# The attention's projections, values and output projection, each issued as two halves in neighbouring rounds

## The reference

```python
x = L0_attn_x
x = x + _L0_attn_ref(_layernorm(x, axis=-1), ...)   # softmax attention, 16 heads of 8 channels
x = x + _L0_ffn_ref(_layernorm(x, axis=-1), ...)    # ternary weights, 128 -> 512 -> 512 -> 512 -> 128
x = x + _L1_attn_ref(_layernorm(x, axis=-1), ...)   # gated linear attention, 8 heads, a scan over tokens
x = x + _L1_ffn_ref(_layernorm(x, axis=-1), ...)    # router, 3 of 8 experts per sequence
```

```python
Q = x @ wq + bq; K = x @ wk + bk; V = x @ wv + bv
Q = Q.reshape(B * H, S, D); K = K.reshape(B * H, S, D); V = V.reshape(B * H, S, D)
scores = jnp.einsum('bqd,bkd->bqk', Q, K) / jnp.sqrt(jnp.float32(D))
attn = jax.nn.softmax(scores, axis=-1)
ctx = jnp.einsum('bqk,bkd->bqd', attn, V).reshape(B, S, E)
out = ctx @ wo + bo
out = out + x
```

## Time and profile before

| | |
|---|---|
| Median of 3 runs | 1133.3 us (1132.64, 1133.3, 1139.46) |
| The profiled execution's own time | 1130.58 us |
| Its span in the profile | 1128.7 us |
| TensorE busy | 1018.0 us (90%) |
| ScalarE busy | 823.8 us (73%) |
| VectorE busy | 642.6 us (57%) |
| GpSimd busy | 369.6 us (33%) |
| Granted TensorE clock, mean | 0.97 of full |

### The profile page before, as it was taken

How to read it: one execution, slowest core, us unless ns; L and a number is a source line. 1 busy time by engine, 2 the same in 40 slices (tenths; PEclk the granted TensorE clock), 3 DMA queues, 4 the chain that set the end, 5 groups by cost and what they waited for, 6 DMA issues and landing times.

```text
span 1128.7 us, 16760 instructions
## 1 busy us (share of the span) xinstructions
PE 1018.0 (90%) x5970; PEld 508.5 (45%) x5970; DVE 642.6 (57%) x1173; ACT 823.8 (73%) x1108; POOL 369.6 (33%) x317
## 2 busy tenths in 40 slices
PE   2799999999999999999697888788588899999998
PEld 1233333333333333333275555465255536666667
DVE  3121444526344444313453899999999999986200
ACT  2599999999999999999457577566667576555541
POOL 1000010101000010100143677898678755755100
PEclk8699999999999999999899899899899999999999
DMA  5765462635455462610101101000000111111200
GB/s 126 121 121 110 82 119 61 123 66 105 78 104 97 85 107 53 119 35 15 33 1 36 33 8 39 29 10 19 19 27 12 57 57 44 41 48 29 63 22 20
DMA packets 99677, 66.91 MB, mean 59 GB/s; under 512 B 62532, under 2 KB 85860, under 8 KB 97508
## 3 DMA queue, kind: packets, MB, share of 16 engines
q1 hardware_dynamic: 99552, 65.34, 27.9%
q10 hardware_dynamic: 24, 0.25, 0.1%
HBM read 46.41 MB, written 18.87 MB: 58 GB/s over the span
## 4 chain that ended last, share of the span: by engine, by line
PE 64%; DVE 15%; ACT 6%; POOL 5%; issue 4%; SPq 3%; DMA 3%; ACTq 0%; DVEq 0%; POOLq 0%
PE PS L1458 26%; PE PS L1443 15%; PE PS L1629 6%; DVE R L1270 6%; PE PS L1618 5%; PE PS L1492 3%; POOL R L871 3%; DVE R L1261 3%; SPq L788 2%; PE PS L1387 1%; DVE RB L1223 1%; PE PS L1532 1%; PE PS L1556 1%; PE PS L1565 1%; PE PS L1373 1%
## 5 line engine op out<-in xcount | busy, mean ns | idle before, releaser
L908 ACT ACTIVATE R<-PS 128x1024 f32<-128x1024 f32 x512 | 474.4, 1085 | 61.4 <-PE PS L1443 60.7
L1458 PE MATMUL PS<-R 128*32 128x512 f32 x2048 | 315.2, 610 | 1.4 <-issue 1.4
L871 POOL TENSOR_TENSOR R<-R 128x512 f32<-128x512 f32 x128 | 212.3, 1674 | 55.5 <-DVE R L1270 30.1
L1270 DVE TENSOR_TENSOR_SCAN R<-R 128x512 f32<-128x512 f32 x128 | 209.2, 1635 | 0.0
L1443 PE MATMUL PS<-RA 34*128 34x512 f32 x1024 | 190.0, 449 | 19.2 <-DMA RA<-QD 18.6
L1492 PE MATMUL PS<-RB,WR 128*128 128x512 f32 x640 | 172.4, 413 | 20.5 <-DVE R L1229 12.5
L1443 PEld LDWEIGHTS PS<-RA 34*128 34x128 f32 x1024 | 77.5, 187 | 216.3 <-issue 194.5
L1492 PEld LDWEIGHTS PS<-RB,WR 128*128 128x128 f32 x640 | 120.9, 192 | 64.9 <-DVE R L1229 14.5
L1458 PEld LDWEIGHTS PS<-R 128*32 128x32 f32 x2048 | 68.0, 108 | 106.2 <-issue 94.2
L857 POOL TENSOR_TENSOR RB<-R,RB 128x512 fp32r<-128x512 f32 x48 | 74.8, 1562 | 83.3 <-ACT RB L918 73.9
L847 POOL PARTITION_ALL_REDUCE R<-R x8 | 3.0, 374 | 290.6 <-DVE R L1110 290.6
(11 more groups left out here) (139 smaller groups left out, 1041.3 us busy)
## 6 DMA issues: line engine op xcount, KB each, us to landing
RA<-QD SPq DMA_DIRECT2D x256, 64.0 KB
QD<-RA SPq DMA_DIRECT2D x128, 64.0 KB, 2.1
RA<-QD SPq DMA_DIRECT2D x64, 128.0 KB
OD<-R SPq DMA_DIRECT2D x128, 32.0 KB, 2.1
R<-OD SPq DMA_DIRECT2D x128, 32.0 KB
VD<-RC SPq DMA_DIRECT2D x16, 256.0 KB, 2.2
RC<-VD SPq DMA_DIRECT2D x128, 32.0 KB
WP<-in_Wa SPq DMA_DIRECT2D x12, 256.0 KB, 3.1
```

The source lines that it names most:

```text
L871: pool.tensor_tensor(st, st, Qc[b % 2], ALU.mult).then_inc(S["qh"], 1)
L908: act.activation(PR[u % 4], bank(2 * s, 1024), ACT.Exp, scale=SC).then_inc(S["exp"], 1)
L1270: dve.tensor_tensor_scan(st, Ac[k], st, CS[:, v:v + 1] if k else 0.0, ALU.mult, ALU.add).then_inc(S["scanned"], 1)
L1458: op = pe.matmul(bank(ob)[c:c + 32, :], VAF[b % 2][:, at:at + 32], PR[u % 4][:, 512 * h:512 * h + 512], start=(j == 0), stop=(j == 7), til ...
```

## The change

Each of the three larger side steps becomes two. The first half is a new step that stands one round before the old one (keys 4, 10, 13 and 18 before keys 5, 11, 14 and 19), with the waits; the second half stays at the old key, writes the rest of the same bank and signals VectorE as before. The Q and K projections are cut at column 256, the values at group 4 of 8, the output projection after 2 of its 4 parts. Where the steps stand outside the rounds (block 0's preparation, block 7's closing) the two halves follow each other directly.

```diff
--- before.py
+++ after.py
@@ -137,8 +137,11 @@
 
         return {
             3: lambda bk: self.add("turn_in", b, bk, self.xn[b]),
+            4: lambda bk: self.add("split_1", b, 1, bk),
             5: lambda bk: (self.add("split", b, 1, bk), self.add("keep", b, 1, 0, 4)),
+            10: lambda bk: self.add("split_1", b, 0, bk),
             11: lambda bk: (self.add("split", b, 0, bk), self.add("keep", b, 0, 0, 4)),
+            13: lambda bk: self.add("values_1", b, bk),
             14: lambda bk: (self.add("values", b, bk), self.add("flag", b)),
             15: lambda bk: self.add("load_pair", 4 * b),
             16: lambda bk: self.add("load_pair", 4 * b + 1),
@@ -168,6 +171,7 @@
 
         return {
             13: lambda bk: self.add("divide", b),
+            18: lambda bk: self.add("project_1", b, bk),
             19: project,
             21: residual,
             23: norm,
@@ -179,8 +183,10 @@
         self.add("pads", 0)
         self.norm_in(0)
         self.add("turn_in", 0, 1, self.xn[0])
+        self.add("split_1", 0, 1, 2)
         self.add("split", 0, 1, 2)
         self.add("keep", 0, 1, 0, 1)
+        self.add("split_1", 0, 0, 3)
         self.add("split", 0, 0, 3)
         self.add("keep", 0, 0, 0, 1)
         for w in (1, 0):
@@ -190,6 +196,7 @@
             self.add("keep", 0, w, 2, 4)
         for n in (1, 2, 3):
             self.add("load_pair", n)
+        self.add("values_1", 0, 4)
         self.add("values", 0, 4)
         self.add("flag", 0)
         self.add("pads", 1)
@@ -453,9 +460,10 @@
     def stream_a(self):
 
         last = self.close(7)
-        for key in (13, 19, 21, 23, 27):
+        for key in (13, 18, 19, 21, 23, 27):
             last[key](6)
-            yield
+            if key != 18:
+                yield
 
 
     def rest(self):
@@ -1380,23 +1388,35 @@
                 transpose4(XN[b % 3], bk).then_inc(S["xt_ps"], 1)
                 emptied[bk] = ("xt", b + 1)
 
-            def split(b, w, bk):
+            def split_1(b, w, bk):
                 need.wait_ge("small_in", 64)
                 need.wait_ge("xt", b + 1)
                 room(bk)
-                pe.matmul(bank(bk), wA[:, w, :], xtblock(b), start=True, stop=True).then_inc(S["qk_ps"], 1)
+                pe.matmul(bank(bk, 256), wA[:, w, :], xtblock(b)[:, 0:256], start=True, stop=True)
+
+            def split(b, w, bk):
+                pe.matmul(bank(bk)[:, 256:512], wA[:, w, :], xtblock(b)[:, 256:512], start=True,
+                          stop=True).then_inc(S["qk_ps"], 1)
                 emptied[bk] = ("qk_f", split_no(b, w))
 
-            def values(b, bk):
+            def values_of(b, bk, g):
+                t0 = 512 * b + 64 * g
+                for c in range(2):
+                    op = pe.matmul(bank(bk)[64 * c:64 * c + 64, 64 * g:64 * g + 64], XT[:, t0:t0 + 64],
+                                   view(wA[:, 2, :], (16, 8), (1, 8), at=8 * c), start=True, stop=True,
+                                   tile_position=(0, 64 * c))
+                return op
+
+            def values_1(b, bk):
                 need.wait_ge("small_in", 64)
                 need.wait_ge("xt", b + 1)
                 room(bk)
-                for g in range(8):
-                    t0 = 512 * b + 64 * g
-                    for c in range(2):
-                        op = pe.matmul(bank(bk)[64 * c:64 * c + 64, 64 * g:64 * g + 64], XT[:, t0:t0 + 64],
-                                       view(wA[:, 2, :], (16, 8), (1, 8), at=8 * c), start=True, stop=True,
-                                       tile_position=(0, 64 * c))
+                for g in range(4):
+                    values_of(b, bk, g)
+
+            def values(b, bk):
+                for g in range(4, 8):
+                    op = values_of(b, bk, g)
                 op.then_inc(S["v_ps"], 1)
                 emptied[bk] = ("va", b + 1)
 
@@ -1462,13 +1482,19 @@
             def finish(pr):
                 emptied[6 + pr % 2] = ("ctx_copied", pr + 1)
 
-            def project(b, bk):
-                k = b % 2
+            def project_of(b, bk, i):
+                return pe.matmul(bank(bk)[:, 128 * i:128 * i + 128], CT[b % 2][:, 128 * i:128 * i + 128], wA[:, 3, :],
+                                 start=True, stop=True)
+
+            def project_1(b, bk):
                 need.wait_ge("ctx", b + 1)
                 room(bk)
-                for i in range(4):
-                    op = pe.matmul(bank(bk)[:, 128 * i:128 * i + 128], CT[k][:, 128 * i:128 * i + 128], wA[:, 3, :],
-                                   start=True, stop=True)
+                for i in range(2):
+                    project_of(b, bk, i)
+
+            def project(b, bk):
+                for i in range(2, 4):
+                    op = project_of(b, bk, i)
                 op.then_inc(S["proj_ps"], 1)
                 emptied[bk] = ("y_sum", b + 1)
 
@@ -1632,8 +1658,8 @@
                     op.then_inc(S["zone_ps"], 1)
                     emptied[bk] = ("x4", b + 1)
 
-            does = dict(turn_in=turn_in, split=split, values=values, attend=attend, guard=guard, scores=scores, weigh=weigh,
-                        finish=finish, project=project, turn=turn, ternary_begin=ternary_begin, gate_mm=gate_mm,
+            does = dict(turn_in=turn_in, split_1=split_1, split=split, values_1=values_1, values=values, attend=attend, guard=guard, scores=scores, weigh=weigh,
+                        finish=finish, project_1=project_1, project=project, turn=turn, ternary_begin=ternary_begin, gate_mm=gate_mm,
                         hid_mm=hid_mm, down=down, turn_b=turn_b, first_c=first_c, proj_c=proj_c, replica=replica,
                         gather=gather, mean_mm=mean_mm, out_c=out_c, turn_c=turn_c, route_1=route_1, route_2=route_2,
                         zone_up=zone_up, zone_down=zone_down)
```

## The result

| | kernel before | changed kernel |
|---|---|---|
| Median | 1133.33 us (6 runs, 1132.64 to 1139.46) | 1146.05 us (6 runs, 1137.1 to 1149.09) |
| Profiled execution | 1130.58 us, span 1128.7 | 1147.21 us, span 1145.4 |
| TensorE matmuls | 5970 | 6002 |

The ratio is 1.0095, with an interval of 1.0067 to 1.0123: **12.7 us or 1% slower by the medians, clear of noise**, where I had forecast 1133.8 us with 1141 as the upper end.

The account below looks back on a forecast made before the run. ScalarE was taken as the bound. Halved splits +0.4 us, values -0.2 and projections +0.3 summed to +0.5, everything else 0; on the median of 1133.3 us that gave 1133.8 us, range 1127.5 to 1141.

Parts of the forecast that it names:

- What bounds the kernel: In the attention rounds ScalarE is the bound, 0.917 us an exponential; TensorE has only 0.17 us to spare each round.
- What a half costs TensorE: Half side steps on TensorE, entry and exit included: split 0.63 us, values 0.61, output projection 0.65.
- How much the neighbouring round hides: First half finds a 0.15 us lead, second about 0.17; a pair costs 0.94 (split), 0.90 (values), 0.98 us (projection).
- The two cancel: Per cut side step, one more entry and exit (0.14 to 0.20 us) offsets one more lead (0.17); sum +0.5 us.
- only the columns cost: Rival: halves take 0.53 to 0.545 us on TensorE, each pair gains 0.17; 4.8 us faster, 1128.5 us; chance 0.12.
- the halves hide wholly: Rival: TensorE has a 0.6 us lead in both rounds; 25.8 us less, 1107.5 us; chance 0.04.
- the second half finds no lead: Rival: all 28 second halves lose their whole length; +4.8 us, 1138.6, or 1141.4 with 0.73 us split halves; chance 0.12.
- What moves with it: First halves take over the waits a round earlier, on transposed block, banks and context; no added wait, 0 us.
- Instruction loads: Rival: 32 more matmuls shift TensorE's instruction-load stalls, 1.8 us each; seven more needed for 1% slower; chance 0.04.
- The median and the range: Whole kernel: difference put on the median of 1133.3 us, giving 1133.8; range 1127.5 to 1141 us.

Follow-up runs that it names:

- experiment 4: Never-executed instructions added in block 0's jumped-over guard body: 40 to the changed kernel, 1135.44 us; 95 to the kernel before, 1136.98 us; both against 1133.74.
- experiment 5: Never-executed instructions in guard bodies of blocks 0, 2, 4, 6: kernel before (62, 22 each) 1132.73 us; changed kernel (48, 6 each) 1130.38 us; both against 1133.23.
- the kernel of values and projection: Changed kernel with splits (Q and K projections) whole again, only values and output projection in halves: 1134.32 against 1133.74 us, ratio 1.0003.
- the kernel of whole steps placed as in the changed one: Kernel before with 8 never-executed instructions added to every block's jumped-over guard body: 1145.76 against 1133.74 us, ratio 1.0102.

## Why the prediction was wrong, point by point

- **What bounds the kernel** was right. ScalarE ends an exponential every 0.917 us, a side step costs its length less 0.15 us, and TensorE regains 0.17 us a round.
- **What a half costs TensorE** was right: 0.63, 0.61 and 0.65 us forecast, 0.63, 0.62 and 0.64 in the chain. Entry and exit are paid twice. The Trainium skill ("TensorE: Matmul & The Clock Gate", Back-to-back issue gap) gives a spacing by columns plus 2.5 ns and no term for entry and exit. By columns alone a split half would be half of the whole step's 1.06, 0.53 us; the trace is against that.
- **How much the neighbouring round hides** was right: 0.94, 0.90 and 0.98 us a pair forecast, 0.93, 0.90 and 0.97 measured. "The two cancel" stands, and the rivals "only the columns cost", "the halves hide wholly" and "the second half finds no lead" are all refuted by these numbers.
- **What moves with it** held in all that I named: no wait on the transposed block, on a bank or on the context. The step that failed is the one that I did not name there. I counted the change's instructions for their time, and not for their place.
- **The rival "Instruction loads"** had the right suspect and the wrong size, and that decided it. I wrote that the new instructions "shift where such loads fall among the DMAs", took a stall for luck at +-1.8 us, wanted seven more of them for 1%, and gave it 0.04. Three more long ones and a longer first were enough: in the changed kernel four stalls cost 20.4 us of ScalarE time, 5.1 each, because they are up to twice as long as the one of the earlier trace rows and because the clock falls behind them for one to three rounds, at 1.18 us for a whole one. And they were no luck: two blocks of tokens come to 2282 instructions before and 2298 after, nearly nine blocks of code (2304), so the odd blocks' jumps all stand at nearly the same place in a code block. Before, that place drifted by 22 from one odd block to the next, 22, 44, 66, 88 left, and left the danger after block 3; the halves bring 16 of the 22, and 6, 12, 18, 24 are left. This could have been counted before the change was timed.
- **The Trainium skill** was cited for the sentence that suited me. "Runtime: NRT & Kernel Launch", Instruction fetch mechanics, says that crossing a block of 16 KiB, 256 instructions, is mostly hidden, and further that a taken branch whose target lies outside the current window of two pages forces a load and a stall. The first holds here: without jumps no stall is seen at any crossing from the 18th exponential to the end of the attention. The second names the right cause, but not the place: in the 24 stalls the target lay in the next block, TensorE ran what was left of it, 2 to 44 instructions, and stood at the beginning of the one after; at the target itself it stood in the two long stalls of experiment 4, in block 7 of experiment 5 and in two shorter ones (0.77 and 0.90 us). I had used the first sentence as an argument against the rival and passed over the second, which would have pointed at the guards.
- **The median and the range.** I put the forecast on the median of 1133.3 and took 1141 from the costs of the halves, none of which came; nothing in the range stood for a mechanism that repeats in every second block.

## What to carry to other kernels

Where a long unrolled program jumps over code, count its instructions: the distance from the landing to the next block of 256 instructions, and from the beginning of a block to the jump, decided here over up to 9 us of the critical engine at a jump, the slow rounds included, and any edit ahead of it moves them all. Before a small slowdown is blamed on an edit, put the same number of instructions into a place that is never executed, and see whether the old kernel slows down as well. Cutting a step into neighbouring pieces only pays when one more lead is worth more than one more entry and exit; here the lead was 0.17 us, and entry and exit 0.14 to 0.20.

## What the runs showed of the hardware that I had not expected

- TensorE runs dry at the same numbers in seven kernels here: 24 stalls of 0.7 us or more end at a matmul whose number in the compiled program leaves 194 when divided by 256, 1.3 to 1.7 us after a load of 16 KB on the instruction queue has ended.
- TensorE goes on 3.3 to 5.2 us after the jump in 23 of those 24, and 7.3 in one. A jump with 50 to 60 instructions or more behind it (0.076 us each in the rounds) mostly hides that; with 44, ScalarE lost 1.6 us in the profile of the kernel of values and projection and 0.6 in that of the kernel before: the load began 2.7 us after the jump in the one and 1.1 in the other.
- The length of a stall did not decide whether the clock fell. In the 27 stalls of 1.2 us or more behind jumps, TensorE's granted clock was 0.50 after 17, among them one of 1.47 us, for up to six slow rounds; it stayed at 1.00 after 10, among them one of 2.63 us (the kernel of whole steps placed as in the changed one has both kinds: about six slow rounds after block 7's 2.37 us, none after block 3's 2.63).
- The kernels with jumps vary more from run to run: without the guard all 12 runs of the whole steps lay between 1125.57 and 1132.07 us, with it the kernel before lay between 1127.87 and 1142.55 in 22 of 23 on the same chip. Late loads and the falling clock could make that spread; no run shows it by itself.
